# First attention: one TensorE loop per batch, Q's second part in the other bank, reciprocals and evictions moved within a unit

## The reference

```python
def _L0_attn_ref(query, Wq, Wk, Wv, Wp, bp):
    B, N, D = query.shape
    H, _, E = Wq.shape
    scale = 1.0 / jnp.sqrt(jnp.asarray(E, query.dtype))
    q = jnp.einsum('bnd,hde->bhne', query, Wq) * scale
    k = jnp.einsum('bmd,hde->bhme', query, Wk)
    v = jnp.einsum('bmd,hde->bhme', query, Wv)
    logits = jnp.einsum('bhne,bhme->bhnm', q, k)
    attn = jax.nn.softmax(logits, axis=-1)
    out = jnp.einsum('bhnm,bhme->bnhe', attn, v)
    out = jnp.swapaxes(out, -1, -2).reshape(B, N, E * H)
    return jnp.dot(out, Wp) + bp
...
x = L0_attn_query
x = _layernorm(x + _L0_attn_ref(x, L0_attn_Wq, L0_attn_Wk, L0_attn_Wv, L0_attn_Wp, L0_attn_bp), axis=-1)
```

## Time and profile before

| what | us |
|---|---|
| median of 3 runs (1135.82 to 1137.63) | 1137.58 |
| the profiled execution's own time | 1134.84 |
| its span, first to last instruction | 1133.0 |
| first attention, about | 0 to 737 of the span |
| one turn of the loop (from 359.98 to 402.48) | 42.50 |

### The profile page before, as it was taken

How to read it: one execution, slowest core, us unless ns; L and a number is a source line. 1 busy time by engine, 2 the same in 40 slices (tenths; PEclk the granted TensorE clock), 3 DMA queues, 4 the chain that set the end, 5 groups by cost and what they waited for, 6 DMA issues and landing times. The chain is left out here.

```text
span 1133.0 us, 25664 instructions
## 1 busy us (share of the span) xinstructions
PE 1035.1 (91%) x7995; PEld 858.1 (76%) x7995; DVE 851.2 (75%) x1703; ACT 699.1 (62%) x1323; POOL 651.9 (58%) x667
## 2 busy tenths in 40 slices
PE   6889999999999999999999999867997599999996
PEld 4668888888888888888888888736685477777774
DVE  5867877877877877877877877454775568989896
ACT  4556666666666666666666666554444487766764
POOL 4156766766766766766766766601131167777772
PEclk9999999999999999999999999988898799999998
DMA  5233533533533533533533533020000011212111
GB/s 123 67 78 75 118 77 80 117 77 80 117 77 80 115 79 80 115 79 80 115 79 80 114 80 80 4 69 1 1 1 1 19 59 57 93 56 74 56 38 38
DMA packets 57578, 80.12 MB, mean 71 GB/s; under 512 B 26500, under 2 KB 38592, under 8 KB 56512
## 3 DMA queue, kind: packets, MB, share of 16 engines
q1 hardware_dynamic: 55324, 79.10, 29.6%
q10 hardware_dynamic: 2220, 0.59, 0.3%
HBM read 19.56 MB, written 1.11 MB: 18 GB/s over the span
## 5 line engine op out<-in xcount | busy, mean ns | idle before, releaser
L596 POOL TENSOR_TENSOR probs_lo<-probs 128x512 f16<-128x512 f32 x384 | 392.9, 1040 | 248.1 <-ACT probs L439 246.8
L460 DVE TENSOR_REDUCE maxes<-bank_m 128x1 f32<-128x512 f32 x512 | 348.7, 688 | 83.8 <-PE bank_m L268 77.2
L439 ACT ACTIVATE probs<-bank_s 128x512 f32<-128x512 f32 x512 | 304.7, 600 | 87.3 <-PE bank_s L356 62.2
L349 PE MATMUL bank_s<-qa,ka 128*128 128x512 f32 x512 | 218.2, 426 | 2.9 <-DVE v_parts L507 2.5
L268 PE MATMUL bank_m<-ka,qa 128*128 128x512 f32 x512 | 211.8, 414 | 4.7 <-DMA ka<-tk_lo 2.4
L356 PE MATMUL bank_s<-qb,kb 65*128 65x512 f32 x512 | 206.0, 402 | 1.4 <-DMA qb<-negmax 1.4
L291 PE MATMUL bank_o<-v_now,probs 128*128 128x129 f16 x2048 | 200.7, 220 | 1.3 <-DVE probs_lo L536 1.3
L291 PEld LDWEIGHTS bank_o<-v_now,probs 128*128 128x128 bf16 x2048 | 175.4, 97 | 21.9 <-issue 18.4
L1347 POOL TENSOR_TENSOR hidden_lo<-rectified,hidden_hi 128x512 fp32r<-128x512 f32 x112 | 155.6, 1406 | 61.0 <-ACT hidden_hi L1492 50.1
L268 PEld LDWEIGHTS bank_m<-ka,qa 128*128 128x128 f32 x512 | 158.7, 310 | 36.9 <-DVE maxes L460 12.7
L287 PE MATMUL bank_o<-v_now,probs_lo 128*128 128x65 f16 x2048 | 184.7, 193 | 0.0
(11 more groups left out here) (250 smaller groups left out, 1691.9 us busy)
## 6 DMA issues: line engine op xcount, KB each, us to landing
qa<-tq_hi SPq DMA_DIRECT2D x64, 256.0 KB, 4.0
v_now<-v_parts SPq DMA_DIRECT2D x32, 260.0 KB, 2.3
ka<-tk_hi SPq DMA_DIRECT2D x32, 256.0 KB, 2.9
ka<-tk_lo SPq DMA_DIRECT2D x32, 256.0 KB, 4.9
kb<-tk_hi SPq DMA_DIRECT2D x32, 256.0 KB, 5.0
qb<-tq_lo SPq DMA_DIRECT2D x32, 256.0 KB, 5.1
gates_on_all<-gate_rows SPq DMA_DIRECT2D x8, 1024.0 KB, 4.7
e_raw<-in_L_ffn_ew_dram SPq DMA_DIRECT2D x16, 256.0 KB, 2.9
```

Source lines behind the costliest of these rows:

```text
L349: nc.tensor.matmul(bank_s[u % 2][:], ka[h][:, ks], qa[h][:, qs], start=True, stop=False)
L439: nc.scalar.activation(probs[:, c, u, :], bank_s[u % 2][:], ACT.Exp, scale=SCALE).then_inc(exp_done, 1)
L460: nc.vector.tensor_reduce(maxes[:, j // 2, j % 2:j % 2 + 1], bank_m[j % 2][:], AX.X, ALU.max).then_inc(m_reduced, 1)
L596: nc.gpsimd.tensor_tensor(probs_lo[:, c, u, :], p, hi, ALU.subtract).then_inc(lo_pool, 1)
```

## The change

The diff does five things, all in the first attention.

1. TensorE's loop is cut in two (one for each batch, 6 and 8 turns), so that the token columns of a projection are constants; the last of the 15 turns stands behind the loops, written out, on every engine.
2. In that last turn (`no_next`) the projections, their evictions, the loads of weights and their staging are left out.
3. Part 1 (Q's second part) goes to `bank_x0` instead of `bank_x1` (`PART_BANK`); `x0_use` and `part_use` count the uses anew.
4. On VectorE the reciprocals come last in units 3 and 7, behind the unit's low half, and `add_y` and `make_lo` come ahead of the low half.
5. On ScalarE the evictions of the V products come behind the unit's exponential instead of ahead of it.

```diff
+    PART_BANK = (1, 0, 1, 1)
...
-        def over_steps(eng, step, before, after):
+        def over_steps(eng, step, before, after, stretches=((0, PAIRS_ALL - 2),)):
+
+            def turn(i, lo):
+                step(i, 2)
+                step(i, 3)
+                step(i + 1, 0, lo=lo)
+                step(i + 1, 1, lo=lo)
...
-            with eng.Fori(0, PAIRS_ALL - 1) as i:
-                step(i, 2)
-                step(i, 3)
-                step(i + 1, 0)
-                step(i + 1, 1)
+            for lo, hi in stretches:
+                with eng.Fori(lo, hi) as i:
+                    turn(i, lo)
+            turn(PAIRS_ALL - 2, PAIRS_ALL - 2)
...
-        x0_base = lambda i: 4 * i - 2
-        x1_base = lambda i: 4 * i + 2
+        x0_base = lambda i: 5 * i - 2
+        x1_base = lambda i: 3 * i + 2
...
                     if (s, u) in PROJECT_AT:
...
-                        project(w, ch, i + 1, 1, x1_base(i) + k)
+                        project(w, ch, i + 1, PART_BANK[k], part_use(k, i), 0 if first else (lo + 2) // PAIRS)
...
+            over_steps(pe, step, before, after, [(max(b * PAIRS - 2, 0), (b + 1) * PAIRS - 2) for b in range(B)])
...
                 for u in range(UNITS):
+                    if (s, u - 1) in PROJECT_AT and not no_next(i):
...
+                        take_part(w, ch, PART_BANK[k], part_use(k, i) + 1)
+                    n = 32 * i + 8 * s + u
+                    act.wait_ge(s_filled, n + 1)
+                    nc.scalar.activation(probs[:, c, u, :], bank_s[u % 2][:], ACT.Exp, scale=SCALE).then_inc(exp_done, 1)
                     if u == 0 and not (first and s < 2):
...
                         for qt in GROUPS_AT[u - 1]:
                             take_o(bi, bs, qt)
-                    if (s, u - 1) in PROJECT_AT:
...
-                        take_part(w, ch, 1, x1_base(i) + k + 1)
-                    n = 32 * i + 8 * s + u
-                    act.wait_ge(s_filled, n + 1)
-                    nc.scalar.activation(probs[:, c, u, :], bank_s[u % 2][:], ACT.Exp, scale=SCALE).then_inc(exp_done, 1)
...
                         reduce(m[2], MAX_N * m[1] + m[2])
+                    if not first and s < 2 and u == Y_AT + 1:
+                        add_y(i - 1, s, x0_use(i, s) + 2)
+                    if (s, u - 1) in PROJECT_AT and not no_next(i):
+                        w, ch, k = PROJECT_AT[s, u - 1]
+                        make_lo(w, ch, PART_BANK[k], 4 * (i + 1) + k, i if k == 0 else None)
...
-                    if u in GROUPS_AT and not (first and s == 0):
-                        bi, bs = (i, s - 1) if s else (i - 1, 3)
-                        for qt in GROUPS_AT[u]:
-                            invert(bi, bs, qt)
                     if u not in POOL_UNITS[s]:
...
+                    if u in GROUPS_AT and not (first and s == 0):
+                        bi, bs = (i, s - 1) if s else (i - 1, 3)
+                        for qt in GROUPS_AT[u]:
+                            invert(bi, bs, qt)
...
-                    if s == 1 and u == UNITS - 1:
-                        pool.wait_ge(x_filled[1], x1_base(i) + 4)
+                    if s == 1 and u == UNITS - 1 and not no_next(i):
+                        pool.wait_ge(x_filled[1], x1_base(i) + 3)
                         stage(i + 2)
```

More of the change, by code:

```diff
@@ L146, in over_steps @@
             after()
+        no_next = lambda i: isinstance(i, int) and i == PAIRS_ALL - 1
         def max_at(i, s, u, first, last):
@@ L227, in before, with step @@
                 load_v(0, 0)
-            def step(i, s, first=False, last=False):
+            def step(i, s, first=False, last=False, lo=0):
                 if s == 0:
                     load_head(1, i, 0 if first else 32 * i)
-                    load_weights(i + 2)
+                    if not no_next(i):
+                        load_weights(i + 2)
                     load_row(0, 1, 4 * i + 1)
@@ L250, in _, with project @@
         def _(pe):
-            def project(which, c, i, bank, use):
+            def project(which, c, i, bank, use, batch):
                 pe.wait_ge(staged, i + 1)
@@ L255, in project @@
                     pe.wait_ge(x_taken[bank], use)
-                col = ((i // PAIRS) % persist["B"]) * N + c * CH
-                out, xs = bank_x[bank][:], bass.ds(col, CH)
+                col = batch * N + c * CH
+                out, xs = bank_x[bank][:], slice(col, col + CH)
                 nc.tensor.matmul(out, w_lo[which][:], xhi[:, xs], start=True, stop=False)
@@ L376, in after @@
                 for c in range(2):
-                    turn_o(i - 1, c, x0_base(i) + 2 * c)
-                    times_wp(i - 1, c, x0_base(i) + 2 * c + 1)
-            over_steps(pe, step, before, after)
+                    turn_o(i - 1, c, X0_END + 2 * c)
+                    times_wp(i - 1, c, X0_END + 2 * c + 1)
+            B = persist["B"]
+            over_steps(pe, step, before, after, [(max(b * PAIRS - 2, 0), (b + 1) * PAIRS - 2) for b in range(B)])
         @block.scalar
@@ L415, in before, with step @@
                                    bank_v[n % 4][:].rearrange("p (h e) -> p h e", e=E)).then_inc(vhi_done, 1)
-            def step(i, s, first=False, last=False):
+            def step(i, s, first=False, last=False, lo=0):
                 c = s % 2
                 for u in range(UNITS):
+                    if (s, u - 1) in PROJECT_AT and not no_next(i):
+                        w, ch, k = PROJECT_AT[s, u - 1]
+                        if k in (0, 2):
+                            loaded, dmas = (head_in, HEAD_DMAS) if k == 0 else (tail_in, TAIL_DMAS)
+                            for g in (0, 1):
+                                act.wait_ge(loaded[g], dmas * (i + 1))
+                        take_part(w, ch, PART_BANK[k], part_use(k, i) + 1)
+                    n = 32 * i + 8 * s + u
+                    act.wait_ge(s_filled, n + 1)
+                    nc.scalar.activation(probs[:, c, u, :], bank_s[u % 2][:], ACT.Exp, scale=SCALE).then_inc(exp_done, 1)
                     if u == 0 and not (first and s < 2):
```

38 lines of the change are left out of this document (18 added, 20 removed).

## The result

| | us |
|---|---|
| before, median of 4 runs (1133.93 to 1137.63) | 1136.70 |
| changed, median of 4 runs (1116.71 to 1119.00) | 1117.52 |
| ratio of the changed kernel to the one before | 0.984, 95% interval 0.9824 to 0.9855 |
| span of the profiled execution, before and after | 1133.0 and 1115.6 |

The forecast was 1117.5. The forecast for the profiled execution was 1114.8, and that one took 1117.38. The first row of the stretches answers to the earlier trace rows: of 300 us in the loop TensorE is busy for 298.32 instead of 288.54.

A forecast was written before the change was run, and what follows sets the result against it. TensorE's matmuls and standstills were taken to bound the first attention. Terms -33 - 2.8 - 11.7 + 25.6 + 1 = -20.9, with 1 us given back, made 1114.8 us profiled and 1117.5 us for the runs; range 1108 to 1131.

The forecast's parts named there:

- Part 1 in the other bank, with the addition ahead: TensorE's waits ahead of projection parts 1 and 2 go, 2.02 us a turn, 33 us gained in all.
- the stop in step 2: TensorE's maxima's matmul and the one behind it come late through VectorE's backlog, 0.33 + 0.23 us a turn.
- The last turn: Last turn without projections: 12 TensorE matmuls at 0.235 us fall away, a gain of 2.8 us.
- Reciprocals last: VectorE no longer idles for the V product, so TensorE's waits for reductions go: 0.78 us in 15 turns, 11.7 us gained.
- the stop in step 3: A late weight load of the maxima's matmul on TensorE, from VectorE's backlog, costs 0.22 us a turn.
- Evictions behind the exponential: Two ScalarE evictions between exponentials make the second exponential and TensorE 0.32 us late in 80 places, a loss of 25.6 us.
- the slower rival: ScalarE's evictions don't overlap, 0.37 us each: second exponential 0.63 us late, 50.4 us lost, 1141.5 us; chance 8%.
- What is late next: The transfer of `ka` has 0.46 us of slack ahead of its reader's weight load; 0.22 us is left, so it holds.
- rival of late transfers or code: `ka` 0.3 us later costs 0.1 us a turn, new code 1 to 2 us per fetch: 1119 to 1123; chance 10%.
- A loss of half the size: The late exponential falls together with waits TensorE has anyway, so half the loss counts: 1105 us; chance 8%.
- The wait in the other bank: Part 1 waits for VectorE's addition, 0.5 us later than reckoned; half of the 33 us is back: 1134; chance 5%.
- The second exponential later than 0.32 us: Evictions at 0.37 us or late reciprocals on ScalarE add 0.1 to 0.2 us in 80 places: 1125 to 1134; chance 13%.

The follow-up runs named there:

- e9: Kernel before with only part 1's bank, the loops and the last turn changed, VectorE and ScalarE in their old order: 1126.78 us, ratio 0.9909.
- e4: Changed kernel with part 1 put back into its old bank, all else changed: 1132.78 us, ratio 0.9955 to the kernel before.
- e3: Changed kernel with reciprocals back ahead of VectorE's low half and evictions back ahead of the exponential: 1100.10 us, ratio 0.9669 to the kernel before.
- e6: Changed kernel with only VectorE's reciprocals back ahead of the unit's low half: 1115.99 us, ratio 0.9824 to the kernel before.
- e2: Kernel before with one edit, ScalarE's evictions moved behind the exponential: 1152.23 us, ratio 1.0133.
- e1: Changed kernel with only ScalarE's evictions put back ahead of the exponential: 1130.57 us, ratio 0.9935 to the kernel before.
- e5: Changed kernel with each pair of reciprocals split around VectorE's low half and each pair of evictions around the exponential: 1096.28 us, ratio 0.9647 to the kernel before.
- e8: Changed kernel with ScalarE evicting each group twice, first into a tile nobody reads: 1162.29 us, ratio 1.0239 to the kernel before.

## Why the prediction was right, and where it wasn't

**The time and the turn.** 1117.52 us for 1117.5, and a turn of 41.27 for 41.3. The first attention ends 20.4 us sooner, where the sum had 20. That the median fits to a hundredth is luck: the sum was made for a profiled execution, which missed by 2.6 us, as the rest of the span took 3.0 more. The stops that the sum counts are the right ones, but for small ones. Which part of the diff takes which of them away is not, as the next paragraphs say, and that the turn comes out all the same is in part luck too.

**Part 1 in the other bank, with the addition ahead.** Both waits went, as the rows of after show, 2.02 us a turn. But the prediction called the bank the cause, and the experiments put more of it on the order of VectorE: the bank in the old order (e9) brings 10 us with the last turn's work, the order in the old bank (e4) lacks 15 us, and both without the rest (e3) bring 37. The prediction's 33 and 2.8 us make 35.8 of these. The order has a gain in them that it was not given, the stop in step 2 (below).

**The last turn.** The changed kernel's last turn, between the V products' steps, is 39.37 us against 42.49: 3.1 us less, while the other turns lost 1.22 (42.49 - 41.27). What it has beyond them is 1.9 us and not the 2.8 of its 12 matmuls. The prediction had one more place there that pays for the evictions, and it is there, in unit 3 of step 1 (0.30 us). It left out that the Wp product, without a projection part just ahead of it, stops for ScalarE's copy of the turned output, 0.18 us in each of steps 0 and 1. These three make 0.66 of the missing 0.9 us (2.8 - 1.9). The first of the two stops:

```profile
677.35 0.74 PEld L331 LDWEIGHTS bank_x<-wp_pair,o_turned 128*128 128x128 f32 x6 [0.34 <-ACT o_turned L420]
```

**Reciprocals last.** This step failed. The maxima's stops went (0.8 us of waits left), but not because the reciprocals moved: with them ahead of the low half again (e6) the time is the same. Of the 0.78 us a turn that the prediction booked here, 0.56 is the stop in step 2. It stays in e2 and e9, which have VectorE's old order, and is gone in e3, where the reciprocals stand as before: the addition ahead of them takes it away, as it fills time in which VectorE waited for the V product. The other 0.22 is the stop in step 3. It is still there in e3 (0.21, and another of 0.18 comes up in unit 6 of step 2, behind a low half of VectorE that took 0.97 us) and gone in e2, e6 and the changed kernel, where TensorE stops for an exponential instead; there a stop is replaced by another one. The move itself brings nothing with the evictions behind the exponential, and costs 30 us with them ahead.

**Evictions behind the exponential.** The mechanism, the five places of a turn and the size of each (0.30 to 0.31 for 0.32) were right, and so was the pace of an eviction: 0.25 us in a row of two, near the 0.265 taken and far from the 0.37 of the slower rival. A ready instruction of ScalarE starts 0.1 us before the recorded end of the one ahead, in every such row above. The prediction took the rule of the Trainium skill ("Advanced Engine Details and Errata", section "The Read-Write Bubble"), that the memory bus isn't pipelined from one instruction to the next, to mean that recorded times can't overlap. They do, by that 0.1 us. That goes against this reading only: the section doesn't say what a recorded time spans, and no run here shows where in it the memory is accessed. Net of what it replaces the move costs 15 us in the kernel before (e2) and 16 us in e6 against e3. With the reciprocals' move it costs 17 us in the changed kernel (e3), instead of 25.6 - 11.7 = 13.9.

**What is late next.** The transfers of `ka` held (3.7 us of waits for them, 2.3 before). One row of maxima came late in the turn in which TensorE enters its second loop: its score matmul started at 340.05, idle for 0.80 us for that transfer, 1.05 us of the turn. Of the eight kernels with two loops, four have such a long turn there (the changed one, e3, e4 and e9, by 0.8 to 1.1 us), and four have none (e1, e5, e6 and e8). In the traces of all twelve kernels every stop of TensorE for a row of maxima of over 0.2 us stands in the first turn of a loop or in the code behind the loops, and none in a turn whose code had run before; the kernel before has one of 1.35 us in its first turn. So the prediction's rival of late transfers or code is likely what is seen here, in a size that hardly counts. That the fetch of the code is the reason is not shown.

```profile
340.05 0.49 PE L376 MATMUL bank_s<-qb,kb 65*128 65x512 f32 x1 [0.80 <-DMA qb<-negmax]
```

**The rivals.** Evictions that don't overlap: no. A loss of half the size: no, in the changed kernel all five places pay. The wait in the other bank: no in the changed kernel, yes in e9, where part 1 waits for the addition (19.2 us in all). The second exponential later than 0.32 us: no, it is 0.29 us late (1.00 for 0.71), and ScalarE waits only 3.4 us for reciprocals.

## What to carry to other kernels

Work that an engine does while the bottleneck is busy with something that doesn't need it is free only at that place: move it between two results that the bottleneck waits for and it costs its full pace. When two moves lean on each other (a reciprocal and the eviction that needs it), take both away and each alone before crediting either. A stop that has gone doesn't tell which of several changes removed it: put each back by itself. A bank is free when its last reader is done, so a second bank helps only together with the place of that reader in its engine's order.

## What the runs showed of the hardware that I had not expected

Spans of GpSimd are rough, but these are steady. GpSimd's low halves took 1108 ns in the mean instead of 1040 (420.1 for 392.9 us in all). Where VectorE's low half and GpSimd's start at the same moment, GpSimd's takes 1.58 us and VectorE's 0.68; where GpSimd was already in the middle of one, VectorE's takes 0.99 us instead of 0.68. In the changed kernel the low half of VectorE comes sooner: 46 times the two start together, and never in the kernel before. It costs nothing here: no instruction of the first attention waits for a low half.

```profile
366.72 0.68 DVE L558 TENSOR_TENSOR probs_lo<-probs 128x512 f16<-128x512 f32 x1
366.72 1.58 POOL L617 TENSOR_TENSOR probs_lo<-probs 128x512 f16<-128x512 f32 x1
368.73 3.04 POOL L617 TENSOR_TENSOR probs_lo<-probs 128x512 f16<-128x512 f32 x3 [0.42 <-ACT probs L450]
371.33 0.99 DVE L558 TENSOR_TENSOR probs_lo<-probs 128x512 f16<-128x512 f32 x1
```
